# Two-layer decoder on one core: latent attention and the dispatch of the rectified experts in one pipeline, expert tiles of 256 rows in plain fp32

## The reference

```python
x = x + L0_attn(layernorm(x))                     # 16 heads
x = x + L0_xattn(layernorm(x), ctx)               # 16 heads, context 128 x 96 per batch
x = x + L0_ffn(layernorm(x))                      # 8 gated experts, top 2, and 2 shared ones
x = x + L1_attn(layernorm(x))                     # 16 heads, causal, rope
x = x + L1_xattn(ctx, layernorm(x), mask)         # latent attention
x = x + L1_ffn(layernorm(x))                      # 8 rectified experts, top 2
```

```python
xn, ln = layernorm(c) * g + b, layernorm(lat) * g + b
q  = ln @ Wq.T;  k, v = concat([xn @ Wkv.T, ln @ Wlkv.T])   # 256 keys, 2 heads of 64
att = softmax(mask(rmsnorm(q) * scale @ rmsnorm(k).T))
out = (att @ v) @ Wo.T + bo
```

```python
logits = xf @ router_w + router_b
topk_w, topk_i = top_k(softmax(logits), 2);  topk_w /= sum(topk_w)
y[e] = relu(xf @ w1[e] + b1[e]) @ w2[e] + b2[e]    # 128 -> 512 -> 128
out = sum over the token's two experts of topk_w * y
```

## Time and profile before

| | us |
|---|---|
| median of 3 runs | 1518.66 (1512.8 to 1520.7) |
| the profiled execution, its own time | 1514.27 |
| its span, first to last instruction | 1512.4 |
| PE busy | 1217.1 (80%), 12300 instructions |
| VectorE, ScalarE, POOL busy | 912.6 (60%), 652.0 (43%), 817.5 (54%) |
| mean granted clock of TensorE | 0.887 |

### The profile page before, as it was taken

How to read it: one execution, slowest core, us unless ns; L and a number is a source line. 1 busy time by engine, 2 the same in 40 slices (tenths; PEclk the granted TensorE clock), 3 DMA queues, 4 the chain that set the end, 5 groups by cost and what they waited for, 6 DMA issues and landing times. The chain is left out here.

```text
span 1512.4 us, 33086 instructions
## 1 busy us (share of the span) xinstructions
PE 1217.1 (80%) x12300; PEld 880.7 (58%) x12300; DVE 912.6 (60%) x2022; ACT 652.0 (43%) x1184; POOL 817.5 (54%) x924
## 2 busy tenths in 40 slices
PE   2899997788888749997999999648899642299991
PEld 1577775555565546664667767448789532266660
DVE  3688785699999644663556665447678533133333
ACT  2354543355454314553444454336566311155550
POOL 3877774365566203343655555277776177355552
PEclk9999998799999857998899999859889655599996
DMA  9910000000000000000000000000000011344426
GB/s 348 380 36 10 2 2 14 14 14 14 26 7 1 2 1 1 1 0 1 2 2 2 3 2 2 7 16 7 12 7 1 1 44 44 109 145 145 136 87 167
DMA packets 58923, 68.55 MB, mean 45 GB/s; under 512 B 13182, under 2 KB 41731, under 8 KB 58640
## 3 DMA queue, kind: packets, MB, share of 16 engines
q1 hardware_dynamic: 52944, 56.92, 11.8%
q0 software_dynamic: 4992, 8.48, 1.7%
q10 hardware_dynamic: 832, 1.07, 0.2%
HBM read 32.76 MB, written 33.42 MB: 44 GB/s over the span
## 5 line engine op out<-in xcount | busy, mean ns | idle before, releaser
L588 DVE TENSOR_REDUCE maxes<-bank 128x8 f32<-128x1024 f32 x192 | 234.4, 1221 | 56.6 <-PE bank L389 55.1
L518 ACT ACTIVATE self_probs<-bank 128x1024 f32<-128x1024 f32 x128 | 129.1, 1022 | 46.0 <-PE bank L422 45.6
L1757 POOL DMA_INDIRECT returned<-relu_y,relu_rows x92 | 90.4, 983 | 95.6 <-DVE relu_y L1686 73.8
L729 POOL TENSOR_TENSOR self_k_hi_m<-self_kq_hi,const 128x512 fp32r<-128x512 f32 x64 | 66.5, 1039 | 78.3 <-ACT self_kq_hi L546 78.3
L525 ACT ACTIVATE self_neg_max<-bank 128x512 fp32r<-128x512 f32 x64 | 38.2, 596 | 150.0 <-PE bank L436 150.0
L1475 ACT ACTIVATE relu_hidden<-bank,cols 128x512 f32<-128x512 f32 x92 | 63.2, 687 | 76.0 <-PE bank L1410 76.0
L1417 PE MATMUL bank<-relu_hidden,relu_w_tile 128*128 128x512 f32 x184 | 93.6, 592 | 0.0
L1677 DVE CAST relu_s_hi<-bank 128x512 fp32r<-128x512 f32 x23 | 15.9, 691 | 118.6 <-PE bank L1396 118.6
L594 DVE TENSOR_SCALAR bank<-bank 128x1024 f32<-128x1024 f32 x64 | 78.2, 1223 | 3.3 <-PE bank L410 3.3
L598 DVE RECIPROCAL self_recip<-bank 128x128 f32<-128x128 f32 x64 | 61.2, 956 | 30.3 <-PE bank L449 27.9
L729 POOL TENSOR_TENSOR causal_q_lo_m<-causal_kq_lo,const 128x512 fp32r<-128x512 f32 x32 | 33.3, 1040 | 84.7 <-PE bank L422 84.7
(11 more groups left out here) (388 smaller groups left out, 3570.1 us busy)
## 6 DMA issues: line engine op xcount, KB each, us to landing
routed<-blank SPq DMA_DIRECT2D x1, 20540.0 KB, 63.9
relu_w_tile<-in_w_ffn SPq DMA_DIRECT2D x23, 512.0 KB, 3.4
relu_rows<-routed SPq DMA_DIRECT2D x23, 260.0 KB, 3.8
relu_back<-returned SPq DMA_DIRECT2D x16, 256.0 KB, 5.3
x_all<-in_x SPq DMA_DIRECT2D x8, 256.0 KB, 8.1
x_before<-x_all SPq DMA_DIRECT2D x8, 256.0 KB, 2.9
out_x<-x_all SPq DMA_DIRECT2D x8, 256.0 KB, 4.4
self_ctx_in<-in_ctx SPq DMA_DIRECT2D x8, 192.0 KB, 2.7
```

What stands on the lines that cost most here:

```text
L518: act.activation(probs[n % 2][:, 2 * pair:2 * pair + 2, :, :].rearrange("p u j q -> p (u j q)"), T[:, 2 * pair * GT:(2 * pair + 2) * GT], ...
L588: dve.tensor_reduce(out.rearrange("p j u -> p u j"), S.rearrange("p (u j k) -> p u j k", u=2, j=U), AX.X, ALU.max, negate=True).then_inc(m ...
L729: pool.tensor_tensor(out[n % 2][:, :, :], src[(n // GB) % 2][:, batch_cols(n)].bitcast(F32).unsqueeze(1).broadcast_to([P, U, P]), slots.un ...
L1757: pool.indirect_dma_start(returned[:, :], bass.IndirectOffsetOnAxis(ap=slots[t % NX][:, b, P:P + 1].bitcast(I32), axis=0), y[t % NY][:, b, ...
```

## The change

The dispatch leaves `relu_experts` and becomes steps of the latent pipeline: `zm`, `zr`, `zs`, `zn` (moments, deviation, shift, rows of a group), `rp` (their copy), `Z`, `zk` (transposes, and their copy out of the bank), and, for units of two groups (the last two groups are units of their own), `L` logits, `R1` the 14 steps, `EX` the exponential, `R` ranks, `GG` gates, `PL` places, and `sc`, the two scatters of a batch. Transposes, logits and ranks use bank TR, as the inputs do; `turn` waits for whoever read it last. The ranks' matmuls are fewer: each adds its counts to the later batches and to the total in one. ScalarE normalises the contexts (`cn`) and rounds inputs and contexts (`hx`, `hc`). The output's bias becomes a matmul of one row into the output's bank; `bo` is gone. The offsets of most steps are new. The tiles have 256 rows (`TT`), so there are 39; both matmuls of a chunk are plain fp32, and the rounding and the rests of weights and rows are gone. The lists of tiles lie in buffers outside both blocks.

```diff
-N_TILES = 2 * B * P // GT + E1 - 1
-N_ROUTED = (E1 - 1) * B * P + N_TILES * GT
+TB = 2
+TT = TB * P
+MOST = B * P // TT
+N_TILES = 2 * B * P // TT + E1 - 1
 ROW = P + 2
 BLANKS = 4
+N_ROUTED = -(-((E1 - 1) * B * P + N_TILES * TT) // (P * BLANKS)) * P * BLANKS
...
-        "PE": "K+2 C^8 T+0 m+0 w-1 f+0 y-2 X^9 s+1 P+5 o-1",
-        "ACT": "v+3 sq+3 ax^8 e-1 ac^7 ln^10 oc-2 cp+4 kh+2",
-        "DVE": "mc^12 ss+3 M+0 mx^14 d+2 hc^7 hx^8 sp+0 u+3 kl+2 n-1 a-2",
-        "POOL": "cn^8 rs^11 ql+1 bo^8 iv+3 lx^7 lc^7",
+        "PE": "T+0 m+0 K+2 w-1 R^-15 y-3 L^-14 f+0 Z^-16 P+5 C^10 o-1 X^9 s+2",
+        "ACT": "zn^-16 cp+4 zk^-17 cn^11 ax^8 ac^9 ln^10 sq+4 kh+2 hc^9 hx^8 e+0 v+5 oc-1 rp^-20 EX^-14",
+        "DVE": "zs^-12 sp+0 d+2 M+1 GG^-15 n-1 a-3 mx^14 mc^13 u+3 kl+2 ss+4 PL^-15 R1^-14 zm^-8",
+        "POOL": "ql+0 zr^-11 iv+2 lc^6 sc-24 rs^11 lx^6",
...
+        for n in range(-14, B + 24):
             for step in ORDERS["latent"][engine].split():
-                name = step.rstrip("+-^0123456789")
+                name = step[:min(step.find(c) for c in "+-^" if c in step)]
                 once = step[len(name)] == "^"
-                first = n + int(step[len(name) + once:])
-                if 0 <= first < B and not (once and first % GB):
-                    yield name, (first // GB if once else first)
+                batch = n + int(step[len(name) + once:])
+                if not 0 <= batch < B:
+                    continue
+                if not once:
+                    yield name, batch
+                elif name in ("L", "R", "R1", "EX", "GG", "PL"):
+                    if batch in LAST:
+                        yield name, LAST[batch]
+                elif batch % GB == 0:
+                    yield name, batch // GB
...
             def up(t, c):
                 i = C1 * t + c
                 if c == 0:
-                    pe.wait_ge(s_lo_done, t + 1)
-                    pe.wait_ge(w_lo_done, t + 1)
+                    pe.wait_ge(s_done, t + 1)
+                    pe.wait_ge(w_in[t % NW], 16 * (t // NW + 1))
                 if i - 1 > 0:
                     pe.wait_ge(hidden_done, i - 1)
-                mine = slice(c * P, (c + 1) * P)
-                hi, lo = w_hi[t % 2][:, mine], w_lo[t % 2][:, mine]
-                pe.matmul(HT[i % 2][:, :], hi, s_hi[t % 2][:, :], start=True, stop=False)
-                pe.matmul(HT[i % 2][:, :], hi, s_lo[t % 2][:, :], start=False, stop=False)
-                pe.matmul(HT[i % 2][:, :], lo, s_hi[t % 2][:, :], start=False, stop=True).then_inc(hidden_made, 1)
+                pe.matmul(HT[i % 2][:, 0:TT], w_tile[t % NW][:, c * P:(c + 1) * P], s[t % 2][:, :], start=True, stop=True)\
+                    .then_inc(hidden_made, 1)
...
-                pe.matmul(YT[t % 2][:, :], w_tile[t % NW][:, F1 + c * P:F1 + (c + 1) * P], hidden[i % C1][:, :],
+                pe.matmul(YT[t % 2][:, 0:TT], w_tile[t % NW][:, F1 + c * P:F1 + (c + 1) * P], hidden[i % C1][:, :],
...
-                dve.tensor_copy(s_hi[t % 2][:, :], TI[:, :]).then_inc(s_hi_done, 1)
-                dve.wait_ge(s_hi_done, t + 1)
-                dve.tensor_tensor(s_lo[t % 2][:, :], TI[:, :], s_hi[t % 2][:, :].bitcast(F32), ALU.subtract)\
-                    .then_inc(s_lo_done, 1)
+                dve.tensor_copy(s[t % 2][:, :], TI[:, 0:TT]).then_inc(s_done, 1)
...
-                sp.wait_ge(scattered[i], 16 * B)
-            sp.wait_ge(listed, 3)
...
+        def turn(engine, name, i):
+            before = [use for use, number in tr_uses.items() if number == tr_uses[name, i] - 1]
+            for use, j in before:
+                if use in ("X", "C"):
+                    engine.wait_ge(affine_done[use], j + 1)
+                elif use == "Z":
+                    engine.wait_ge(x_t_done, j + 1)
+                elif use == "L":
+                    engine.wait_ge(routed_step, ROUTE * j + 1)
+                else:
+                    engine.wait_ge(placed, PLACE * j + 5)
...
+            def transpose_rows(G):
+                pe.wait_ge(rows_made, G + 1)
+                turn(pe, "Z", G)
+                for b in range(GB):
+                    mm = pe.transpose(TR[:, b * P:(b + 1) * P], rows[G % 4][:, 0, b, 0:P], ident)
+                mm.then_inc(rows_transposed, 1)
+            def make_logits(u):
+                pe.wait_ge(x_t_done, UNITS[u][-1] + 1)
+                turn(pe, "L", u)
+                for i, G in enumerate(UNITS[u]):
+                    for b in range(GB):
+                        c = (i * GB + b) * E1
+                        mm = pe.matmul(TR[:, c:c + E1], x_t[G % 2][:, b * P:(b + 1) * P], router, start=True, stop=True)
+                mm.then_inc(logits_made, 1)
+            def count_earlier(u):
+                pe.wait_ge(routed_step, ROUTE * u + 13)
+                turn(pe, "R", u)
+                n = batches(u)
+                pe.matmul(TR[:, 0:n * E1], cr[:, C_BEFORE:C_BEFORE + P],
+                          both[:, 0:n, :].rearrange("p b e -> p (b e)"), start=True, stop=False)
+                for b, start, end in [(0, 1, n), (0, n, n + 1)] + [(b, b + 1, n + 1) for b in range(1, n)]:
+                    mm = pe.matmul(TR[:, start * E1:end * E1].rearrange("p (b e) -> p b e", e=E1),
+                                   cr[:, C_FULL:C_FULL + P],
+                                   both[:, b, :].unsqueeze(1).broadcast_to([P, end - start, E1]),
+                                   start=False, stop=b == n - 1)
+                mm.then_inc(counted, 1)
...
-                pe.matmul(M[:, 0:P], o_t[n % 2][:, :], wo, start=True, stop=True).then_inc(out_projected, 1)
+                pe.matmul(M[:, 0:P], one[:, :], bo, start=True, stop=False)
+                pe.matmul(M[:, 0:P], o_t[n % 2][:, :], wo, start=False, stop=True).then_inc(out_projected, 1)
...
+            def input_hi(name, G):
+                act.wait_ge(affine_done[name], G + 1)
+                if G > 1:
+                    act.wait_ge(projected, GB * (G - 1))
+                out, src = (x_hi, xf) if name == "X" else (c_hi, cf)
+                act.activation(out[G % 2][:, :], src[:, :], ACT.Copy).then_inc(hi_done, 1)
...
+            def normalise_context(G):
+                act.wait_ge(rstd_done, G + 1)
+                if G > 0:
+                    act.wait_ge(transposed["C"], G)
+                for b in range(GB):
+                    op = act.activation(cn[:, b, :], ctx_in[:, b, :], ACT.Identity, scale=rstd[:, b:b + 1],
                                         bias=shift_ln[:, b:b + 1])
-                op.then_inc(x_normal, 1)
+                op.then_inc(c_normal, 1)
...
+            def make_rows(G):
+                act.wait_ge(z_shift_done, G + 1)
+                rows_free(act, G)
+                for b in range(GB):
+                    op = act.activation(rows[G % 4][:, 0, b, 0:P], x_of(GB * G + b), ACT.Identity,
+                                        bias=z_shift[G % 2][:, b:b + 1], scale=z_rstd[G % 2][:, b:b + 1])
+                op.then_inc(rows_made, 1)
+            def repeat_rows(G):
+                act.wait_ge(rows_made, G + 1)
+                act.activation(rows[G % 4][:, 1, :, 0:P], rows[G % 4][:, 0, :, 0:P], ACT.Copy).then_inc(repeated, 1)
+            def keep_rows(G):
+                act.wait_ge(rows_transposed, G + 1)
+                if G > 1:
+                    act.wait_ge(logits_made, [G - 2 in unit for unit in UNITS].index(True) + 1)
+                act.activation(x_t[G % 2][:, :], TR[:, :], ACT.Copy).then_inc(x_t_done, 1)
...
+            def scatter(n):
+                G = n // GB
+                u = [G in unit for unit in UNITS].index(True)
+                pool.wait_ge(placed, PLACE * (u + 1))
+                pool.wait_ge(labelled, 2 * UNITS[u][-1] + 2)
+                pool.wait_ge(repeated, G + 1)
+                b = n - GB * UNITS[u][0]
+                for k in range(2):
+                    pool.indirect_dma_start(
+                        routed[:, :], bass.IndirectOffsetOnAxis(ap=place_i[u % 3][:, k, b:b + 1], axis=0),
+                        rows[G % 4][:, k, n % GB, :], None).then_inc(scattered[G % 4], 16)
...
-                pool.tensor_tensor(x, x, bo.unsqueeze(1).broadcast_to([P, GB, P]), ALU.add).then_inc(biased, 1)
...
+                sp.wait_ge(scattered[i], SENT * len(range(i, NG, 4)))
```

670 lines of the change are left out of this document (273 added, 397 removed).

## The result

The changed kernel takes 1436.38 us (median of 4 runs, 1434.43 to 1439.97) against 1515.73 for the kernel before (4 runs, 1512.03 to 1520.7): a ratio of 0.9476, 95% interval 0.9453 to 0.9500, 79 us less. The forecast was 1459. Run again beside two of the experiments it took 1438.17 (ratio 0.9493, 0.9441 to 0.9546). Its first profiled execution has a span of 1434.2 us, the second 1436.0.

What follows compares the result with a forecast made beforehand. No engine bounded the whole span: waits paced early attention, TensorE later attention and experts, POOL's scatters the dispatch. Stage ends summed to 1454.5, 1456 with the span's 1.9; between that and the median's 4.4 offset, 1459 us, own range 1436 to 1479.

Steps and rivals of the forecast that it cites:

- (a): Attention's first addition to x: one iteration deeper, 5.5 us more, 3 back from the contexts' DMA wait; at 1036.
- (b): Attention, batches 0 to 18: 5.5 us each, 99 in all, to 1135; ends 5.0 and 6.6 each.
- (c): Attention's other 13 batches, now carrying the dispatch: 64 us, ending near 1200, 12 later; ends 1180 and 1235.
- (d): Scatters left behind attention: 42 of 64, 1.26 us apart, 53.0 plus 1.3, to 1254; ends 1249 and 1282.
- (e): Last scatter's following slot to experts' first transposes: 7.9 us as before plus 0.7 for a block border; 1263.
- (f): Experts' stage: 39 tiles at 4.12 us, 160.7 against 165.6; with both ends 168.1, to 1431.
- (g): Fetch and sum of the returned rows after the experts: as before, 23.4 us, to 1454.5.
- 1** (ring and bank, slower): Attention's shared bank and ranks' waits cost the ring's sum; at 7.5 us per iteration, 1535; chance 0.06.
- 2** (half tiles beside their columns): Experts' half tiles meet a once-per-tile wait 39 times instead of 23; at 5.2 us per tile, 1501; chance 0.11.
- 3** (the port): Scatters hold up VectorE's two-tile steps by 1.0 us each; attention ends 22 later, 1481; chance 0.08.
- 4** (scatters all stay behind): The lag of 24 keeps every scatter behind attention: 22 more at 1.26 us, 1487; chance 0.05.
- the busiest engine filled: Attention, batches 0 to 18: low end of the pace forecast, 5.0 us per batch.

Runs made afterwards that it cites:

- e1: Changed kernel with every dispatch step 32 iterations later, so all of it stands behind attention's last addition; 1472.45 us.
- e2: Changed kernel with expert tiles of 512 rows instead of 256, still plain fp32; 1465.07 us.
- e4: Changed kernel with contexts normalised in the same iteration as the next group's moments, as before, still by ScalarE; 1458.68 us.
- e5: Changed kernel with contexts normalised by POOL again, in the iteration in which ScalarE did it; 1472.74 us.
- e10: Changed kernel with a unit's 14 routing steps dealt to two iterations, and ranks, gates and places one iteration later; 1436.71 us.
- e6: Changed kernel with the dispatch four iterations nearer to the additions, scatters 20 instead of 24 batches behind; 1473.54 us.
- e8: Changed kernel with every routing unit one group instead of two, scatters 12 instead of 24 batches behind, shorter statistics lag; 1476.83 us.
- e11: Changed kernel with scatters 20 instead of 24 batches behind, POOL's deviations still three iterations behind the statistics; 1441.54 us.
- e3: Changed kernel, tiles still 256 rows, with up-matmuls as three rounded ones and weights and rows split, as before; 1450.23 us.
- e12: Changed kernel with scatters 20 behind, deviations' slack kept, six routing units instead of five, y ahead of the ranks; 1438.64 us.

## Why the prediction was right, and where it was off

The direction and the order of the gains were right, and so was what each of the three large parts does (e1, e2, e4). The gain was 79 us and not some 60 between medians, 76.5 and not 58 between profiles. 1436.38 lies only 0.4 us inside the lower end of the forecast's own range, 1436 to 1479, and it is a sum of errors of both signs: -10.6 (a), -6.2 (b), +6.2 (c), +0.7 (d and e), -6.4 (f), -1.4 (g). Step by step, against the second profile:

(a) First addition. Forecast 1036, measured 1025.5. The wait on the contexts' DMA had been taken for 3 us of the fill; with it back (e4) the fill is 5.0 longer. The extra iteration of depth did not show as 5.5: in the fill no engine is full (TensorE 31 of 52 us). The clock was at its lower level for some 45 us of the fill before, 27 now and 41 in e4; how much of the gain is the clock's is not shown.

(b) Batches 0 to 18. Forecast 5.5 each, measured 5.16. The term that was mis-sized is TensorE's. I added new work to its 5.15 per batch of the earlier trace rows, but these had been measured at a mean clock of 0.91: some 20 of the 106 us at the lower level, 18.5 of them busy. At the full clock that would be about 4.6 per batch, an estimate that halves the 18.5. With the wait gone TensorE is busy 93.00 of 93 us at 1.00, 5.16 per batch with the new work in it. The bias matmul in it takes 0.41 and not 0.25 (two instructions, L1770). That TensorE became the bound, "the busiest engine filled", was given as the low end; it was the case. e4 shows that the wait on the DMA was the cause (17.6 us of wait, 18.3 of time), e5 that ScalarE's part is needed as well.

(c) Batches 18 to 31. Forecast 64, measured 70.2. The dispatch costs attention 15.8 in all (e1). 13.2 of it lie in three steps from the first routing on and in three from the second on. These six in the second profile, then the same six in e1 (columns as in the earlier trace rows):

```profile
1118.28:1136.25 17.97, 17.93 (x131) 16.26 (x131) 16.58 (x59) 10.24 (x35) 10.99 (x12) 1.00 0.03 9
1161.71:1183.48 21.77, 20.81 (x90) 18.09 (x90) 8.84 (x42) 4.47 (x14) 9.28 (x11) 0.53 0.08 27
...
1111.30:1126.00 14.70, 14.70 (x106) 13.35 (x107) 10.70 (x31) 9.07 (x30) 7.62 (x8) 1.00 0.00 1
1149.50:1161.34 11.84, 10.46 (x63) 8.25 (x63) 3.91 (x14) 2.75 (x9) 0.26 (x1) 0.95 0.01 1
```

At the first routing TensorE does not stand, and its clock is full: 3.3 us more, for 25 matmul instructions more. The logits take 1.78 from their start to the next matmul's, the ranks 1.20. VectorE's 14 steps in a row (first and last):

```profile
1120.62 0.22 DVE L2028 TENSOR_TENSOR latent_logits<-bank,rows 128x64 f32<-128x64 f32 x1
...
1123.96 0.17 DVE L2058 TENSOR_TENSOR latent_behind<-latent_top 128x8 f32<-128x8 f32 x1
```

They make the one step long, 8.89 with VectorE busy 8.27 of it, but not what the routing costs (e10). At the second routing 9.9 us are lost, and there the larger part goes with the clock, which is at its lower level from about 1163 to 1259. The weighing of the values, and the ranks, at the first routing and at the second:

```profile
1122.99 1.00 PE L1758 MATMUL bank<-latent_v,latent_probs 128*128 128x65 f32 x8
1124.11 1.15 PE L1693 MATMUL bank<-latent_both,const_r 128*128 128x56 f32 x9
...
1166.65 1.81 PE L1758 MATMUL bank<-latent_v,latent_probs 128*128 128x65 f32 x8
1168.43 2.06 PE L1693 MATMUL bank<-latent_both,const_r 128*128 128x56 f32 x9
```

From the first to the last addition TensorE is busy 160.9 of 163.0 us, in e1 144.0 of 147.0: attention is longer by what TensorE is busy longer. At most 11 us of that is the clock (29 us at the lower level and not 6; an estimate), and 6 the logits and ranks of two units. The work per batch was forecast well: the first 8 of the 13 batches took 43.4, 44 in the forecast. The last five took 26.7 and not 20, and the term that the forecast put at nothing is the lower clock. What made it fall is not shown: from 1152.7 to 1163.3 the trace has TensorE standing nowhere, and the last it did before was the logits. (a) to (c) together: attention 0.5 longer, not 12.

(d) The tail. 24 scatters stand before the last addition (22 forecast), 40 behind it: last addition to the slot after the last scatter 52.8, forecast 54. Measured in one piece with (e) the step was right within 1 us, because two errors cancel: this one is 1.2 too long, (e) 2.3 too short.

(e) Last scatter to first transposes: 12.2, forecast 9.9. From the last scatter's start to SP's first issue there are 7.4 us, where the earlier trace rows has 3.6, and the first transposes come 3.0 later than before. The forecast put 0.7, at most 3, on the border between the blocks; that the border is what costs the 3.0 is likely, but no run is without it.

(f) The experts. 3.90 per tile, not 4.12; 39 tiles make 8.6 less. The 0.08 per chunk that I kept from the rounded groups isn't there in plain ones: eight matmuls at 0.43 and two pairs of transposes at 0.22, not 0.18. That is 0.1 over the low end. Some 2 us come back at the two ends: the first tiles, at the lower clock until 1259, cost 1.8 and not 0.7 more than their pace, the last one 0.9, and from the last matmul to the fetch 5.9 pass and not 5.5. DMA is as forecast: the hardware queue is busy 54.2% of the stage in the first profile, 2.1 us of 3.90 per tile (2.2 of 4.12 was 53%).

The fetch and sum (g) took 1.4 less than before.

The rivals. **1** (ring and bank, slower): no. Its mean of 7.5 per iteration did not come, and its own waits, for the shared bank and for the ranks, aren't there: TensorE stands 2.1 us in all from 1118 to 1188. e6 to e8 show another ring, POOL in order behind VectorE's statistics, which costs attention 43 to 68 us. What keeps it out is not the lag of 24 but the three iterations between the statistics and the deviations: with these kept, a lag of 20 costs 8 (e11). **2** (half tiles beside their columns): no; TensorE was busy 140.00 of 140. A wait once per tile is what the split has (e3). **3** (the port): no. VectorE's two-tile step beside a scatter and beside POOL's arithmetic, second profile:

```profile
1141.45 0.96 POOL L2215 DMA_INDIRECT routed<-latent_rows,latent_place_i  x1 [0.30 <-issue]
1141.74 0.55 DVE L1947 TENSOR_TENSOR latent_unit<-latent_kq,latent_inverse 128x384 f32<-128x384 f32 x1
...
1035.75 1.29 POOL L2178 TENSOR_TENSOR latent_x_lo<-latent_xf,latent_x_hi 128x512 fp32r<-128x512 f32 x1
1035.91 1.54 DVE L1947 TENSOR_TENSOR latent_unit<-latent_kq,latent_inverse 128x384 f32<-128x384 f32 x1
```

0.55 beside a scatter, six times of six, which is its time alone; 1.54 beside a subtraction on POOL, as in the earlier trace rows. The Trainium skill, "SBUF — State Buffer", Who interferes with whom, says that a VectorE instruction with two SBUF inputs contends with a GpSimd instruction that reads SBUF, and that tensor_tensor was not seen to stall GpSimd's DMAs, for a reason that it calls inferred. The trace agrees with both: 1.54 beside the subtraction, and for these scatters neither side waits (954 to 1230 ns, median 958, as in the earlier trace rows). The prediction had left out the second half, which speaks against rival 3. **4** (scatters all stay behind): no, 24 of 64.

What stays open: why the clock falls in the second routing; what the smaller parts are worth, since the bias as a matmul, the rounding on ScalarE and the fewer matmuls of the ranks were never taken back alone (the bias costs TensorE, the bound, 0.41 a batch); what VectorE's unnamed waits are (13.3 and 7.7 us in one of two profiles of the same kernel, four in e12, none in the others), and why the latent phase begins anywhere between 967 and 982 us. The granted clock from 528 to 582 us differs from run to run with the same instructions (0.50 before, 0.62 and 0.59 in the two of after, 0.55 in e12), but the start does not follow it.

## What to carry to other kernels

Read the granted clock beside each busy time. Here TensorE's busy time in a stage with waits held 18.5 us at the lower clock; with the waits gone the same work took less and new work fitted in. The other way round, a wait of TensorE came back about twice: in e6 it stood 21.7 us more and was busy 25.5 more.

In an order written out by hand, look at who stands behind a moved step in the same engine's list, and at how many iterations lie between it and what it waits for. One iteration in place of three cost attention 48 us here (e6). Before a long step is explained by the engine that works in it, add up the bound engine's own work over the steps around it: dealing VectorE's 14 steps out changed which step was long, and not their sum.

Once attention was full, each further part of the tail that was moved into it came back one for one (e11: 8.3 less, 8.2 more; e12: 13.0 less, 15.1 more).

## What the runs showed of the hardware

An indirect scatter issued by POOL does not hold up a VectorE instruction that reads two tiles of SBUF (0.55 us beside it, six of six; 0.52 to 0.56 alone), while a subtraction of POOL that has just begun does (1.54). In tiles of 256 rows, three rounded up-matmuls per chunk cost TensorE the same as one plain fp32 matmul (3.86 and 3.90 busy per tile). The same eight matmuls of 65 columns take 1.00 us at a clock of 1.00 and 1.81 at 0.50. A bias of one row as a plain fp32 matmul of 128 columns takes 0.41. A one-off wait of up to 13.3 us on VectorE can stand in a single profile: compare two before one is explained.
